# Attention with a gated mixture of experts on one core: the exact path decided from the weights, rows and logits in one product, gates by tanh, first scores inside the prologue

## The chip, the cores and the metric

The kernel runs on one core of one Trainium2 chip. The metric is the device time of one execution in microseconds (us); lower is better. Engines are named as in the profile: PE (matrix products and transposes), ACT (activations), DVE and POOL (vector work), SP (starts most DMAs). A tile name such as `exps` is the program's own.

## What is computed

`x` has 4 batches of 1024 tokens of 128 numbers. With `xn = layernorm(x)`:

```python
p = xn @ Wv.T + bv                      # 16 heads of 8; queries = keys = values = p
s = softmax(p_h @ p_h.T / sqrt(8)) @ p_h  # per batch and head, heads joined
s = s @ Wo.T + bo
z = layernorm(xn)
w = top 2 of softmax(z @ rW + rb), scaled to sum 1     # 8 experts
mixed = sum_e w[e] * (gelu(z @ W1[e] + b1[e]) @ W2[e] + b2[e])   # 128 -> 256 -> 128
out = x + s * silu(xn + mixed)
```

## The kernel before, in words

**The steps.** The 64 pairs of a batch and a head are done four heads at a time: 16 units. A unit has 2 halves of the queries (512 columns) and 8 tiles of 128 keys, so 16 steps, 256 steps in all. In a step PE computes scores (`scores`, L1142: four products into one of three PSUM pairs, two heads each), ACT takes their exponential (L686, two instructions of 128x1024), and PE multiplies by the values of the step two steps back (`values`, L1154). DVE turns and divides each finished half.

**The table of uses.** All other PSUM work goes through one bank, `bank_f`, and a table (`timetable`) says in which step PE makes which use of it: `turn` and `project` of a finished unit, `count` (how many tokens ahead chose the same expert), `bias`, `up` (first layer of four slots of tokens), `down` (second layer). A step has at most one use, but for a *burst*: right after the gelu of a half of the tokens, eight `down` uses stand in a single step. `MOE_AT`, the step of the first `up`, is 31. `GELU_AT`, `GATHER_AT`, `SILU_AT` and `Y_AT` follow from the table: the steps at which ACT does the gelus, POOL starts to fetch expert outputs, ACT does the silus, and DVE finishes a unit's output.

**The prologue.** Before the first step, eight blocks of 512 tokens go through a chain: DVE computes mean and inverse root (`norm1`, a chain of small instructions in which each waits for the one before), ACT normalises (L627), PE transposes (`turn_x`, L1066), ACT copies, PE multiplies by `Wv` (`project_p`, L1073) and by the router (L1078, logits), ACT adds the bias (L642), PE transposes back (`turn_p`, L1086) and sums squares per head (L1092). POOL splits each block into a high and a low part (`split`, L575 square, L578 cast, L580 subtract), and SP stores the parts and the squared norms `m_blk` to `p_dram` (L406, L408), from where `load_head` and `load_stabiliser` (L391 to L398) bring four heads into `k_ring` and `q_ring`, five DMAs a head. DVE copies the rows (L743, `keep_p`) and reduces the norms to a maximum (L746); ACT halves them (L648).

**The exact path.** The score of a token with itself, half its squared norm, serves as the bound that keeps the exponential small. When the largest squared norm `m2` passes 400, a loop computes true row maxima instead. `m2` is known after the last block (L784); PE, DVE and SP then each load it into a register and branch over that loop (PE L1108).

**Routing.** After the branch DVE scales the logits with the second layernorm's factor (`norm2`, `keep_logits` L763), picks the two experts and ranks the tokens (L839 to L855). PE's `count` in step 3 (L1183) waits for that, ACT's small exponential (L677) in step 2 for a part of it. POOL then scatters the tokens' rows to `z_dram`, SP loads expert weights and gathers 512 rows at a time into `z_ring` (L490).

**The queue of SP** is in program order: loads, then per block stores and head loads, then the branch, then at fixed steps whatever the table says.

## Time and profile before

| | us |
|---|---|
| median of 3 runs | 654.75 (652.24 to 656.18) |
| the profiled execution, its own time | 647.5 |
| its span | 645.5 |
| PE busy | 582.8 (90% of the span) |
| ACT busy | 547.7 (85%) |
| DVE busy | 237.8 (37%) |
| POOL busy | 156.7 (24%) |
| mean granted PE clock, share of full | 0.917 |
| first exponential of the first step | 72.69 after the span's start |

Times inside the span are counted from its start. Busy shares are means over stages with different limits: PE is not busy at its peak where its clock is halved, and an engine that is busy beside another may cost nothing. An idle time in a row is put in brackets with what ended it; "issue" is time in which the profile shows no wait.

### The profile page before, as it was taken

The page shows a single profiled execution, that of the slowest core. Times are in us where ns is not written, and L with a number is a line of the kernel's source. Part 1 is how long each engine was busy: PE and PEld are TensorE (multiplying, and loading weights), DVE is VectorE, ACT ScalarE, POOL GpSimd, SP SyncE. Part 2 cuts the span into 40 slices and gives each one's busy share as a digit, 9 for nine tenths or more (in the row PEclk, how much of TensorE's full clock was granted, in tenths as well). Part 3 has the DMA queues.
Part 4 walks back from the last instruction along what each step waited for, and adds up shares of the span by engine and source line. Part 5 has one row for each costly group of instructions (what it writes and reads, how often), then busy time and mean ns, then how long its engine had stood idle before and what let it go on. Part 6 is the DMA issues. An engine that isn't in the chain of part 4 may idle for free.

```text
span 645.5 us, 11510 instructions
## 1 busy us (share of the span) xinstructions
PE 582.8 (90%) x4036; PEld 243.4 (38%) x4036; DVE 237.8 (37%) x677; ACT 547.7 (85%) x595; POOL 156.7 (24%) x172
## 2 busy tenths in 40 slices
PE   5668599979999996999999999999799979999976
PEld 5445142324433444443434343433434434323311
DVE  7555567613333331132222222222234434224323
ACT  2453589959998999799999999999789989999994
POOL 5335147777400000000000000005256000077300
PEclk9856589979999996799999999999589989999978
DMA  7125698765565443435334635333175436232101
GB/s 223 42 81 152 224 302 272 231 170 154 131 155 138 111 100 101 130 77 140 103 98 115 156 93 155 75 88 98 38 196 154 140 95 187 66 91 59 34 17 49
DMA packets 103883, 81.33 MB, mean 126 GB/s; under 512 B 51371, under 2 KB 95806, under 8 KB 103230
## 3 DMA queue, kind: packets, MB, share of 16 engines
q1 hardware_dynamic: 99726, 72.16, 41.3%
q0 software_dynamic: 4096, 8.40, 4.6%
q8 instruction: 33, 0.54, 0.3%
q14 instruction: 28, 0.23, 0.1%
HBM read 57.97 MB, written 28.32 MB: 134 GB/s over the span
## 4 chain that ended last, share of the span: by engine, by line
PE 67%; ACT 14%; DVE 7%; issue 7%; SPq 4%; DMA 1%; ACTq 0%; DVEq 0%
PE bank_v L1154 30%; PE pair L1142 14%; ACT exps L686 11%; PE bank_f L1200 9%; PE bank_f L1191 7%; PE bank_f L1171 1%; PE pair L1073 1%; DVE rows_in_sb L720 1%; SPq L467 1%; PE bank_f L1078 1%; DVE veps L725 1%; PE bank_f L1167 1%; SPq L468 1%; DVE o_ring L990 1%; ACT xn_tok L627 1%
## 5 line engine op out<-in xcount | busy, mean ns | idle before, releaser
L686 ACT ACTIVATE exps<-pair 128x1024 f32<-128x1024 f32 x512 | 487.6, 1050 | 49.6 <-PE pair L1142 31.1
L1154 PE MATMUL bank_v<-exps,v_tok 128*32 128x512 f32 x2048 | 281.7, 623 | 2.2 <-DVE o_turned L946 1.5
L1142 PE MATMUL pair<-q_ring,k_ring 26*128 26x512 f32 x1024 | 155.5, 510 | 13.9 <-ACT exps L686 8.7
L602 POOL DMA_INDIRECT rows_in_sb<-o_dram,dest_i x64 | 60.7, 948 | 372.8 <-DMA o_dram<-o_ring 336.0
L1142 PEld LDWEIGHTS pair<-q_ring,k_ring 26*128 26x128 f32 x1024 | 61.9, 186 | 113.2 <-ACT exps L686 71.2
L1200 PE MATMUL bank_f<-w_ring,pre 128*128 128x128 f32 x320 | 65.5, 334 | 11.7 <-DVE o_ring L990 6.2
L1200 PEld LDWEIGHTS bank_f<-w_ring,pre 128*128 128x128 f32 x320 | 48.6, 218 | 72.1 <-issue 40.8
L592 POOL DMA_INDIRECT z_dram<-pre,dest_i x64 | 64.2, 1003 | 40.8 <-DVE dest_i L909 21.7
L1191 PEld LDWEIGHTS bank_f<-zT,w_ring 128*128 128x128 f32 x320 | 42.5, 193 | 75.2 <-DVE pre L981 45.1
L981 DVE TENSOR_TENSOR pre<-bank_f,w_ring 128x256 f32<-128x256 f32 x80 | 33.9, 424 | 98.5 <-PE bank_f L1191 98.5
L1154 PEld LDWEIGHTS bank_v<-exps,v_tok 128*32 128x32 f32 x2048 | 41.3, 110 | 68.7 <-ACT exps L686 38.0
L1191 PE MATMUL bank_f<-zT,w_ring 128*128 128x128 f32 x320 | 57.6, 304 | 7.1 <-issue 6.2
L990 DVE TENSOR_TENSOR o_ring<-bank_f,w_ring 128x128 f32<-128x128 f32 x80 | 23.3, 291 | 109.6 <-PE bank_f L1200 108.6
L946 DVE STREAM_TRANSPOSE o_turned<-bank_v 128x512 f32<-128x512 f32 x32 | 22.9, 717 | 92.2 <-PE bank_v L1154 92.2
L627 ACT ACTIVATE xn_tok<-x_tok,shift,rstd 128x128 f32<-128x128 f32 x32 | 13.1, 480 | 12.2 <-DVE shift L727 12.2
L648 ACT ACTIVATE pre<-bank_v 16x512 fp32r<-16x512 f32 x8 | 4.7, 585 | 16.8 <-DVE max_block L746 16.8
L666 ACT ACTIVATE pre<-pre 128x2048 f32<-128x2048 f32 x10 | 18.2, 1896 | 0.0
L1066 PE MATMUL pair<-ident,xn_tok 128*128 128x128 f32 x32 | 7.1, 361 | 12.0 <-ACT xn_tok L627 12.0
L926 DVE STREAM_TRANSPOSE zT<-z_ring 128x512 f32<-128x512 f32 x20 | 14.2, 712 | 9.4 <-DMA z_ring<-z_dram 8.7
L964 DVE TENSOR_TENSOR s_tok<-bank_f,bo_bc 128x256 f32<-128x256 f32 x16 | 6.8, 424 | 27.3 <-PE bank_f L1171 27.3
L575 POOL TENSOR_TENSOR pre<-pre 128x512 bf16<-128x512 f32 x8 | 8.3, 1043 | 33.5 <-ACT pre L642 25.3
L956 DVE COPY attnT<-bank_f 128x256 f32<-128x256 f32 x16 | 6.8, 425 | 25.3 <-PE bank_f L1167 25.3
(130 smaller groups left out, 306.3 us busy)
## 6 DMA issues: line engine op xcount, KB each, us to landing
w_ring<-w_dram SPq DMA_DIRECT2D x80, 192.0 KB
w_ring<-w_dram SPq DMA_DIRECT2D x80, 129.0 KB, 2.1
q_ring<-p_dram SPq DMA_DIRECT2D x56, 104.0 KB
k_ring<-p_dram SPq DMA_DIRECT2D x56, 96.0 KB
z_dram<-s_tok SPq DMA_DIRECT2D x4, 1280.0 KB, 8.7
z_ring<-z_dram SPq DMA_DIRECT2D x80, 64.0 KB
o_dram<-o_ring SPq DMA_DIRECT2D x20, 256.0 KB, 2.3
p_dram<-pre SPq DMA_DIRECT2D x16, 256.0 KB, 2.9
```

Of the source, the lines that this page charges most:

```text
L592: pool.indirect_dma_start(z_dram[h][:, :], bass.IndirectOffsetOnAxis(dest_i[:, h, c, i:i + 1].bitcast(U32), 0), z0[:, h * HT + i, :], None ...
L602: pool.indirect_dma_start(rows_in_sb[:, (h * HT + i) % GATHER_RING, c, :], None, o_dram[h][:, :], bass.IndirectOffsetOnAxis(dest_i[:, h, c ...
L627: ins = nc.scalar.activation(xn_tok[:, t, :], x_tok[:, t, :], ACT.Identity, bias=shift[:, t:t + 1], scale=rstd[:, t:t + 1])
L666: nc.scalar.activation(part, part, ACT.Gelu).then_inc(gelu_done, 1)
L686: nc.scalar.activation(exps[:, g % ES, 2 * half:2 * half + 2, :], pair[(2 * g + half) % 3][:, :, :], ACT.Exp, scale=SCALE).then_inc(exp_do ...
L946: nc.vector.transpose(o_turned[:, qh, :, :], bank_v[:, :].rearrange("p (r s) -> p s r", s=QR)).then_inc(o_turned_ready, 1)
L981: ins = nc.vector.tensor_tensor(pre[:, k, i * HF:(i + 1) * HF].rearrange("p (c t) -> p c t", c=FC), bank_f[:, 0:HF].rearrange("p (c t) -> ...
L990: ins = nc.vector.tensor_tensor(o_ring[:, q % 2, i, :], bank_f[:, 0:D], w2_ring[:, q % 2, i, FC * D:W2W], ALU.add)
L1142: ins = nc.tensor.matmul(pair[h % 3][:, j % 2, :], k_ring[32 * j:32 * j + KROWS, n % 2, kt * P:(kt + 1) * P], q_ring[32 * j:32 * j + KROWS ...
L1154: ins = nc.tensor.matmul(bank_v[32 * j:32 * j + 32, :], v_tok[:, (n // HG) * KT + kt, first:first + 32], exps[:, g % ES, j, :], start=(kt ...
L1191: ins = nc.tensor.matmul(bank_f[:, c * P:(c + 1) * P], w1_ring[:, q % 2, i, c * P:(c + 1) * P], zT[:, q % 2, i * P:(i + 1) * P], start=Tru ...
L1200: ins = nc.tensor.matmul(bank_f[:, 0:D], pre[:, k, (i * FC + c) * P:(i * FC + c + 1) * P], w2_ring[:, q % 2, i, c * D:(c + 1) * D], start= ...
```

## The change

- **The decision.** The largest squared norm is bounded from the weights: PE multiplies `Wv` with itself per head and adds the bias's product, DVE sums absolute values per row (`sum_gram`), PE transposes, DVE takes the maximum (`keep_m2`). PE decides and branches before the first block; the usual prologue stands in the `Else` part. DVE and SP load the same number and branch where they did. For the given weights the largest half row sum is 1.11 and the limit 1.535.
- **Rows and logits in one product.** `rows_p` multiplies the transposed block with `Wv` and the router side by side (128 columns of rows, 8 of logits), four products a block; `turn_p` and the separate logits go. DVE adds the bias (L785) and keeps the logits (L786). The norms' sums (`norms_p`) come three blocks later, and DVE copies them (`keep_n2`) where it reduced and ACT halved.
- **First scores inside the prologue.** The first three score groups stand between the last products of the prologue.
- **Fills.** ACT fills `k_ring` and the zeros where POOL did; POOL's square of a block no longer waits for the sums of the block before.
- **Loads.** All 20 head loads go in a row at block 2, and W1 (1 MB) with two small loads behind the norms of block 3 instead of at the start. `norm2` of both halves moves behind the last `keep_n2`. The 16 tiles of the last `norm1` are cut in two times 8.
- **Table.** First `up` at step 36, bursts of six `down` with two more placed apart; gelus at 87 and 182 (before 81 and 174), fetches at 176 and 228 (170 and 220).
- **Gates.** silu(u) becomes u(1 + tanh(u/2))/2: eight tanh of four tiles each, at steps 187, 192, 198, 204, 239, 244, 250 and behind the last step, with one DVE instruction behind each (`gate`), in place of two silus of 16 tiles at 198 and 248. Units 14 and 15 are both finished behind the last step; before, only 15 was.

```diff
-M2_LIMIT = 400.0
+N2_LIMIT = 400.0
+M2_LIMIT_BITS = int(np.float32(0.99 * N2_LIMIT / (D + 1) / 2).view(np.int32))
-NORMS = ((0, 4), (4, 4), (8, 8), (16, 16))
-WARM = (9, 8)
+NORMS = ((0, 4), (4, 4), (8, 8), (16, 8), (24, 8))
+WARM = (4, 6)
-MOE_AT = 31
+MOE_AT = 36
-BURST = 2
+BURST = 6
...
-        uses[g] = [("down", first + k, i) for k in range(BURST) for i in range(4)]
+        downs = [("down", first + i // 4, i % 4) for i in range(8)]
+        uses[g] = downs[:BURST]
...
+        t = g + 3
+        for what in downs[BURST:]:
+            t = max(t, place(what, t) + 1 - MOE_STEP) + MOE_STEP
...
                 sp.wait_ge(parts_ready, g + 1)
...
+                if g == 2:
+                    for i in range(2):
+                        sp.wait_ge(parts_stored[i], 16 * PARTS)
+                    sp.wait_ge(m_kept[0], 32)
...
+                    for j in range(4):
+                        load_head(0, 0, j, 0, kq_in[0])
+                        load_stabiliser(0, j, kq_in[0])
                 sp.wait_ge(n2_copied, g + 1)
...
+                if g == 3:
+                    sp.dma_start(w1_stage, W1.rearrange("e h f -> h e f")).then_inc(w1_staged, 16)
...
-            pool.memset(k_ring[:, :, :].bitcast(F32), 1.0).then_inc(ring_cleared, 1)
-            pool.memset(s_tok[:, :, :], 0.0).then_inc(zeros_ready, 1)
...
-            def silu(h):
-                act.wait_ge(combined, (h + 1) * HT)
-                part = xn_tok[:, h * HT:(h + 1) * HT, :]
-                nc.scalar.activation(part, part, ACT.Silu).then_inc(gate_ready, 1)
+            def tanh_half(c):
+
+                act.wait_ge(combined, (c + 1) * SILU_TILES)
...
+                nc.scalar.activation(th[:, c % 2, :], part, ACT.Tanh, scale=0.5).then_inc(tanh_ready, 1)
...
+            def keep_n2(g):
                 dve.wait_ge(n2_mm, g + 1)
-                nc.vector.tensor_reduce(max_block[:, g:g + 1], bank_v[0:H, :], X, ALU.max).then_inc(n2_max, 1)
+                nc.vector.tensor_copy(m_blk[:, g, :].bitcast(F32R), bank_v[0:H, :]).then_inc(n2_copied, 1)
...
+            keep_n2(0)
+            norm1(4, *NORMS[4])
+            for g in range(3, NB):
                 keep_p(g)
...
+                keep_n2(g - 2)
+            for g in range(NB - 2, NB):
+                keep_n2(g)
+            for h in range(HALVES):
+                norm2(h)
...
+            with pe.Else():
+                keep_warm(WARM[1])
+                prologue()
+                first_scores(0)
+                rows_p(NB - 1)
+                norms_p(NB - 3)
+                first_scores(1)
+                norms_p(NB - 2)
+                first_scores(2)
+                norms_p(NB - 1)
```

PE at the end of the prologue, before: the last block's way back and its sums (L1092), the transpose of the maxima (L1105, behind DVE's last reduction), the load of `m2` and the branch; the first scores stand behind the skipped loop.

```order
L1086 MATMUL pair<-ident,pre 128x128 [waits p_copied,pT_copied]
L1086 MATMUL pair<-ident,pre 128x128 x3
L1092 MATMUL bank_v<-pre,head_sel 16x512 [waits n2_max,n2_copied,sq_ready]
L1105 MATMUL pair<-ident,max_head 1x16 [waits p_copied,max_head_ready]
L1107 TENSOR_LOAD m [waits m2_ready]
L1108 COMPARE_AND_BRANCH
```

PE at the same place in the change (L1130 projects the last block, L1139 is rows and logits, L1146 the norms' sums, L1179 the scores, in three groups of two heads):

```order
L1130 MATMUL pair<-pre,wv_rw 128x512 [waits pT_copied,xT_copied]
L1179 MATMUL pair<-q_ring,k_ring 128x512 [waits kq_in0,xT_copied]
L1179 MATMUL pair<-q_ring,k_ring 128x512
L1139 MATMUL pair<-wv_rw,pre 128x136 [waits p_copied]
L1139 MATMUL pair<-wv_rw,pre 128x136 x3
L1146 MATMUL bank_v<-w_ring,head_sel 16x512 [waits n2_copied,sq_ready]
L1179 MATMUL pair<-q_ring,k_ring 128x512 [waits pT_copied]
L1179 MATMUL pair<-q_ring,k_ring 128x512
L1146 MATMUL bank_v<-w_ring,head_sel 16x512 [waits n2_copied,sq_ready]
L1179 MATMUL pair<-q_ring,k_ring 128x512 [waits p_copied]
L1179 MATMUL pair<-q_ring,k_ring 128x512
L1146 MATMUL bank_v<-w_ring,head_sel 16x512 [waits n2_copied,sq_ready]
```

The three first score groups moved ahead of the last sums, and between them stand sums that wait for POOL's squares (`sq_ready`) and DVE's copies (`n2_copied`); load and branch are gone from here and stand ahead of the first block.

DVE at the same place, before: `norm2` of the first half (L734 to L738, its middle left out here) stood between the copies of blocks 2 and 3; its last rows and what follows:

```order
L737 TENSOR_TENSOR veps<-veps,rstd 128x16 [waits dve_chain]
L738 TENSOR_TENSOR rstd<-rstd,veps 128x16 [waits dve_chain]
L743 COPY v_tok<-pair 128x4x16x8 [waits p_tr,dve_chain]
L746 TENSOR_REDUCE max_block<-bank_v 16x1 [waits n2_mm]
L734 SCALAR_TENSOR_TENSOR veps<-veps,mv 128x16
L706 TENSOR_SCALAR rstd<-veps 128x16 [waits dve_chain]
```

DVE in the change, from the rows of block 6 to the start of `norm2` (L785 and L786 keep rows and logits, L790 is `keep_n2`, L760 begins `norm2`):

```order
L785 TENSOR_TENSOR v_tok<-pair,rows_in_sb 128x4x16x8 [waits p_mm]
L786 COPY lg_all<-pair 128x32
L790 CAST exps<-bank_v 16x512 [waits n2_mm]
L785 TENSOR_TENSOR v_tok<-pair,rows_in_sb 128x4x16x8 [waits p_mm]
L786 COPY lg_all<-pair 128x32
L790 CAST exps<-bank_v 16x512 [waits n2_mm] x3
L760 SCALAR_TENSOR_TENSOR veps<-veps,mv 128x16
L732 TENSOR_SCALAR rstd<-veps 128x16 [waits dve_chain]
L733 TENSOR_SCALAR rstd<-rstd 128x16 [waits dve_chain]
```

Both chains of `norm2`, 14 instructions each in which every one waits for the one before, stand behind the last three `keep_n2`; the register load and the branch follow them.

SP in the change, from the last two issues of the head loads (L416, L420) on; L428 stores the parts of a block, L439 its norms, L441 is W1:

```order
L416 DMA q_ring<-p_dram 8x1024
L420 DMA q_ring<-p_dram 2x1024
L439 DMA p_dram<-exps 16x512 [waits n2_copied]
L428 DMA p_dram<-z_ring 16x8x512 [waits parts_ready]
L428 DMA p_dram<-o_ring 16x8x512
L439 DMA p_dram<-exps 16x512 [waits n2_copied]
L441 DMA w_ring<-in_L_ffn_W 128x8x256
L442 DMA rb_bc<-in_L_ffn_rb 128x8
L443 DMA bo_bc<-in_L_attn_bo 128x128
L428 DMA p_dram<-z_ring 16x8x512 [waits parts_ready]
L428 DMA p_dram<-o_ring 16x8x512
L439 DMA p_dram<-exps 16x512 [waits n2_copied]
```

Before, one head load of five issues stood behind the stores of each of the blocks 2 to 5, and W1 ahead of all blocks; now the parts of block 3 stand behind all 20 issues, and those of block 4 behind W1 as well.

## Rows read from the trace of the kernel before

**Rows 1.** The page, chain of work that ended last, shares of the span.

```profile
PE 67%; ACT 14%; DVE 7%; issue 7%; SPq 4%; DMA 1%; ACTq 0%; DVEq 0%
```

**Rows 2.** Timeline, PE, first transpose of a block: start us, us, engine, line, op, names, count.

```profile
15.35 0.77 PE L1066 MATMUL pair<-ident,xn_tok 128*128 128x128 f32 x4
```

**Rows 3.** Timeline, DVE, first inverse root, then the statistics of the last 16 tiles.

```profile
4.93 4.77 DVE L725 TENSOR_SCALAR veps<-mv 128x4 f32<-128x4 f32 x1
...
28.50 3.17 DVE L720 BATCH_NORM_STATS2 rows_in_sb<-x_tok 128x6 f32<-128x128 f32 x16
```

**Rows 4.** Timeline, PE, around the branch and the count.

```profile
71.86 1.22 PE L1142 MATMUL pair<-q_ring,k_ring 26*128 26x512 f32 x6 [4.88 <-issue]
...
80.69 0.23 PE L1183 MATMUL bank_f<-pre,earlier 128*128 128x128 bf16 x1
```

**Rows 5.** Timeline, DVE, last norms, first instruction behind the branch, the choice.

```profile
65.88 0.68 DVE L746 TENSOR_REDUCE max_block<-bank_v 16x1 f32<-16x512 f32 x1 [0.35 <-PE bank_v L1092]
...
72.05 0.17 DVE L758 TENSOR_TENSOR rconst<-bank_f,rb_bc 128x8 f32<-128x8 f32 x1 [4.87 <-issue]
...
79.90 0.23 DVE L855 TENSOR_SCALAR pre<-pre 128x128 bf16<-128x128 f32 x1
```

**Rows 6.** Timeline, DVE, first and last of the 14 instructions of a norm2.

```profile
50.79 0.15 DVE L734 SCALAR_TENSOR_TENSOR veps<-veps,mv 128x16 f32<-128x16 f32 x1
...
53.49 0.18 DVE L738 TENSOR_TENSOR rstd<-rstd,veps 128x16 f32<-128x16 f32 x1
```

**Rows 7.** Timeline, POOL, first and last of the three instructions of a split.

```profile
43.27 1.05 POOL L575 TENSOR_TENSOR pre<-pre 128x512 bf16<-128x512 f32 x1 [1.93 <-PE bank_v L1092]
...
44.96 1.28 POOL L580 TENSOR_TENSOR pre<-pre 128x512 fp32r<-128x512 f32 x1
```

**Rows 8.** Timeline, DVE, an instruction of a norm2 beside that split.

```profile
45.15 1.12 DVE L709 SCALAR_TENSOR_TENSOR newton<-rstd 128x16 f32<-128x16 f32 x1
```

**Rows 9.** Timeline, DMA queue of SP: W1 and the last small load.

```profile
7.22 2.52 SPq L369 DMA_DIRECT2D w_ring<-in_L_ffn_W  x1
...
11.41 0.43 SPq L371 DMA_DIRECT2D bo_bc<-in_L_attn_bo  x1
```

**Rows 10.** Timeline, DMA queue of SP: first of five head issues, and the two stores after them.

```profile
45.13 0.30 SPq L391 DMA_DIRECT2D k_ring<-p_dram  x1
...
46.97 1.20 SPq L406 DMA_DIRECT2D p_dram<-pre  x2
```

**Rows 11.** The page, DMA issues: KB each, median us to landing.

```profile
p_dram<-pre SPq DMA_DIRECT2D x16, 256.0 KB, 2.9
```

**Rows 12.** Timeline, PE, ACT and SP around the first up, step 31.

```profile
140.37 1.20 PE L1191 MATMUL bank_f<-zT,w_ring 128*128 128x128 f32 x4 [4.72 <-issue]
...
142.33 1.94 ACT L686 ACTIVATE exps<-pair 128x1024 f32<-128x1024 f32 x2 [5.48 <-PE pair L1142]
145.84 5.17 ACT L686 ACTIVATE exps<-pair 128x1024 f32<-128x1024 f32 x5 [1.57 <-PE pair L1142]
...
135.77 6.50 SPq L490 DMA_DIRECT2D z_ring<-z_dram  x12
```

**Rows 13.** Timeline, ACT and PE, after and in the first burst.

```profile
261.81 1.94 ACT L686 ACTIVATE exps<-pair 128x1024 f32<-128x1024 f32 x2 [3.29 <-PE pair L1142]
...
249.80 1.22 PE L1200 MATMUL bank_f<-w_ring,pre 128*128 128x128 f32 x4 [0.39 <-DVE o_ring L990]
```

**Rows 14.** Groups of ACT by line, 505 to 646 us: count, busy us, mean ns, idle.

```profile
L671 ACT ACTIVATE xn_tok<-xn_tok 128x2048 f32<-128x2048 f32 x2 | 3.8, 1910 | 0.0
L671 ACT ACT_TABLE_LOAD x2 | 2.6, 1283 | 0.0
```

**Rows 15.** Timeline, ACT, first pauses behind the two silus.

```profile
524.80 4.01 ACT L686 ACTIVATE exps<-pair 128x1024 f32<-128x1024 f32 x4 [1.44 <-PE pair L1142]
...
625.58 1.94 ACT L686 ACTIVATE exps<-pair 128x1024 f32<-128x1024 f32 x2 [0.73 <-PE pair L1142]
```

**Rows 16.** Timeline, DVE, first of the two instructions that finish a unit.

```profile
642.37 0.43 DVE L940 TENSOR_TENSOR s_tok<-s_tok,xn_tok 128x256 f32<-128x256 f32 x1
```

More of the change, by code:

```diff
@@ L130, in timetable @@
         t = both("up", k, t)
-    gelu = [burst(0, t)]
-    t = gelu[0] + 2
+    first, t = burst(0, t)
+    gelu = [first]
     t = both("up", QUADS, t)
     t = both("up", QUADS + 1, t)
-    for k in range(BURST, QUADS):
+    for k in range(2, QUADS):
         t = both("down", k, t)
         t = both("up", QUADS + k, t)
-    gelu.append(burst(QUADS, t))
-    t = gelu[1] + 4
-    for k in range(BURST, QUADS):
+    second, t = burst(QUADS, t)
+    gelu.append(second)
+    for k in range(2, QUADS):
         t = both("down", QUADS + k, t)
@@ L259, in build @@
         bank_m = [pair[2][:, i, :] for i in range(2)]
+        p_rows = pair[2][:, :, :].rearrange("p a (t w) -> p (a t) w", w=2 * P)
+        bank_g = [pair[1][:, i, :] for i in range(2)]
         p_dram = nc.dram_tensor("p_dram", [H, HEAD_ROWS, N], F32)
@@ L623, in normalise @@
             def normalise(g):
-                if g != 3 and g <= 4:
-                    act.wait_ge(norm_ready, (1, 2, 3, 3, 4)[min(g, 4)])
+                if (c := {first // TB: c for c, (first, _) in enumerate(NORMS)}.get(g)) is not None:
+                    act.wait_ge(norm_ready, c + 1)
                 for t in range(g * TB, (g + 1) * TB):
@@ L679, in _ @@
                         gelu(h)
-                    if g == SILU_AT[h]:
-                        silu(h)
+                for c in range(SILUS):
+                    if g == SILU_AT[c]:
+                        tanh_half(c)
+                if 2 <= g < 4:
+                    act.wait_ge(m_kept[g - 2], NB // 2 * 16)
                 for half in range(2):
@@ L687, in _ @@
                                          scale=SCALE).then_inc(exp_done, 1)
-            for h in range(HALVES):
-                if SILU_AT[h] >= STEPS:
-                    silu(h)
+            for c in range(SILUS):
+                if SILU_AT[c] >= STEPS:
+                    tanh_half(c)
         @block.vector
@@ L1016, in beside @@
                         scale_w1(part)
+                for c in range(SILUS):
+                    if g == GATE_AT[c]:
+                        gate(c)
                 for n in range(NU - 1):
@@ L1033, in _ @@
                     read_bank(*use)
-            finish_y(NU - 1)
+            for c in range(SILUS):
+                if GATE_AT[c] >= STEPS + VLAG:
+                    gate(c)
+            for n in range(NU):
+                if n == NU - 1 or Y_AT[n] >= STEPS + VLAG:
+                    finish_y(n)
         @block.tensor
@@ L1047, in _ @@
             keep_warm(WARM[0])
[L1048 to L1049 removed]
+            pe.wait_ge(wv_in, 32)
+            nc.tensor.transpose(pair[0][:, 0, 0:D], wv_sb, ident[:, :]).then_inc(wv_tr, 1)
+            pe.wait_ge(wv_copied, 1)
+            nc.tensor.matmul(bank_g[0][:, 0:D], wvT, wvT, start=True, stop=False)
+            nc.tensor.matmul(bank_g[0][:, 0:D], bv_bc[0:1, :], bv_bc[0:1, :], start=False, stop=True).then_inc(gram_mm, 1)
+            pe.wait_ge(rows_in, 16 * 5)
             nc.tensor.transpose(bank_f[:, D:2 * D], wo_sb, ident[:, :])
@@ L1108, in _ @@
             with pe.If(m2_bits > M2_LIMIT_BITS):
+                prologue()
+                rows_p(NB - 1)
+                for g in range(NB - 3, NB):
+                    norms_p(g)
+                pe.wait_ge(p_copied, NB)
                 with pe.Fori(0, NU // 2) as w:
@@ L1131, in _ @@
                 pe.wait_ge(exact_in, NU * 16 * PART_LOADS + 16 * KQ_FIRST)
-            def scores(g, half):
-                n, k = divmod(g, US)
-                qh, kt = divmod(k, KT)
-                h = 2 * g + half
-                if k == 0 and half == 0:
-                    pe.wait_ge(kq_in[n % 2], 16 * (KQ_FIRST + n // 2 * KQ_LOADS))
-                if h >= 3:
-                    pe.wait_ge(exp_done, h - 2)
-                for j in range(2 * half, 2 * half + 2):
-                    ins = nc.tensor.matmul(pair[h % 3][:, j % 2, :], k_ring[32 * j:32 * j + KROWS, n % 2, kt * P:(kt + 1) * P],
-                                           q_ring[32 * j:32 * j + KROWS, n % 2, qh * BLK:(qh + 1) * BLK], start=True, stop=True)
-                ins.then_inc(scores_done, 1)
+                for h in range(3):
+                    first_scores(h)
+            with pe.Else():
+                keep_warm(WARM[1])
+                prologue()
+                first_scores(0)
+                rows_p(NB - 1)
+                norms_p(NB - 3)
[3 more added lines that the diff above has]
+                norms_p(NB - 1)
             def values(g):
@@ L1206, in _ @@
                 if g < STEPS:
-                    scores(g, 0)
-                    scores(g, 1)
+                    for half in range(2):
+                        if 2 * g + half >= 3:
+                            scores(g, half)
                 if g >= VLAG:
```

250 lines of the change are left out of this document (138 added, 112 removed).

## The prediction

> **What bounds the kernel now.** I read the chain of work that ended last first: PE holds two thirds of the span, ACT 14%, and 7% is "issue", waits that nothing in the profile explains [rows 1]. So neither engine is slow as a whole; the loss lies in single holes, and the timelines of PE, ACT, DVE and SP's queue around each idle time show four kinds. (a) The prologue: first transpose of a block at 15.35 [rows 2], last norms read at 66.56 (65.88 + 0.68) [rows 5], then both PE and DVE stand 4.88 and 4.87 us at the branch [rows 4, 5]. (b) Step 31, the first `up`: PE waits 4.72 us and ACT idles 5.48 and 1.57, because SP issued the gather of tokens only from 135.77 [rows 12]. (c) Two bursts, after which ACT idles 3.29 [rows 13]. (d) Two silus with a table load on either side [rows 14].
>
> The durations below come from the profiled execution, 647.5 us, 7.25 (1.1%) under the median 654.75. I put the sum on the median. A difference of 0.5%, 3.3 us, is about what a measurement of this kernel can tell from no change.
>
> **The prologue.** PE must now wait for `m2` before the first block. DVE's first chain was held 4.77 us in its first small instruction [rows 3] while POOL filled the tiles that ACT fills now; without that hold the first two `norm1`, about 4.1 each from 3.6 on, and the small sums between them end near 12.8: `m2`. The branch adds 4.88 [rows 4] and six warming products some 2.6, all estimates from these rows: first transpose at 20.3, 4.9 later than before. That the fills leave POOL gains nothing at the end, since PE's branch is later than the norms either way.
>
> Next, DVE. Before, it reached the statistics of the last tiles at 28.50 [rows 3], 13.2 after the first transpose; now one more slot of PE (about 4, because the norms lag by three blocks) stands ahead, so 37.5. The last `norm1` has 8 tiles: half of 3.17 [rows 3], 0.6 of averages, and a chain of 13 that I take from the 14 of a `norm2`, 50.79 to 53.67 = 2.88 [rows 6]; with one hold by POOL as in [rows 8], 6 us in all: 43.5. Rows of block 3 and norms of block 1 end at 45.2; the store lands about 2 later. Then SP issues 20 loads: five took from 45.13 to 46.97, 1.84 [rows 10], so 7.4, until 54.6. With four landed some 2 later the first scores and exponential come near 57, 15 us earlier than before. That is the gain the eye sees first, and it can't be kept, for the reason that follows.
>
> Behind the loads on SP stand the norms of block 2 (0.6), the parts of block 3 (1.2) and its norms (0.6), each bounded by a store of [rows 10]; then W1 with the two small loads, 7.22 to 11.84 = 4.62 [rows 9]; then the parts of block 4, 0.6 to the issue of the second and 2.9 to landing [rows 11]. That is 65.1. POOL's cast of block 6 waits for it: cast and subtraction 1.92 (a split of 2.97 less its square 1.05 [rows 7]), the square of block 7 1.05, the sums about 0.4 (six products of 512 columns took 1.22 [rows 4]), DVE's copy 0.68 [rows 5], hand-overs 0.2: the last norms are kept at 69.3. Before, at 66.56.
>
> Then, in line on DVE: two `norm2`, before hidden between blocks, now 2 x 2.88 = 5.8; the branch 4.87; routing from 72.05 to 80.13 = 8.08 [rows 5]. The choice is ready at 88.1. ACT's routing exponential, in step 2, and PE's `count`, in step 3, wait for it, and behind them every later score: the hold. Before, PE came to the count at 80.69 [rows 4] with the choice ready. So step 4 starts 7.4 later. PE then has idled for some 10 us. After the idle of step 31 the next pause of ACT was 1.57 [rows 12]; I add that. **Prologue: +9.0.** Bounds: 0 if the choice is ready by 80.7; +13.5 if the parts land 4.5 later (below).
>
> **Step 31.** The first `up` comes at step 36, five steps later; SP's gather, tied to earlier steps, is issued at the same distance from them. Five steps at about 1.9 are 9.5, the wait was 5.48 [rows 12]: 4 us to spare. **-7.0** (5.48 + 1.57). Bounds: 0, if SP falls 4 us behind, and -7.0.
>
> **Bursts.** ACT's 3.29 [rows 13] is waiting for eight `down`. Six leave out two of 1.22 and a pause of 0.39 each [rows 13], 3.2. Those two then take a place in later steps, at most 1.2 each; I take 0.6, since part of it lies beside ACT's exponentials: -2.0 a burst. **-4.0**, bounds 0 and -6.6.
>
> **Gates.** Two silus took 1.91 each, and four table loads (two at L671 and, not shown, two ahead of the next exponential) 1.28 each [rows 14]: 8.9. Behind them ACT idled 1.44 and 0.73 [rows 15]: 11.1 goes. The eight tanh have 512 columns where a silu has 2048: between 0.48, a quarter, and 1.91 [rows 14]; I take 0.6, nearer the quarter. Three in steps that ACT bounds cost 1.8; the first four, where PE sets the pace, some 0.7; the last lies behind the last exponential, beside the last values. **-8.6**; bounds -11.1 and -6.3 (all eight in full). No table load stands beside a tanh in the order of the changed program. DVE's `gate` runs where DVE is mostly idle; if that cover went, each would cost its step at most about 0.9.
>
> **End.** Unit 14 is finished behind the last step too: two instructions of 0.43 [rows 16], and the last gate about 0.2: **+1.1**. The fetches start 8 steps later, and so do their readers; they keep their distance. The one product for rows and logits shortens PE's slots, but the prologue's end is set by SP and DVE: worth 0.
>
> Sum: 9.0 - 7.0 - 4.0 - 8.6 + 1.1 = -9.5. 647.5 becomes 638.0; on the median **645.2**.
>
> **The rivals.**
>
> No hold. If the branches cost little in the change, `m2`'s branch on PE and the one on DVE give 4.8 each back: the choice near 78.5, before PE needs it; prologue 0, time 636.2. Against it: both engines show the wait of 4.9 at the branch [rows 4, 5]; for it: that they waited there over a loop, and the code behind may have been fetched by then. The Trainium skill (Advanced Engine Details and Errata, section Control Flow Timing) gives a compare-and-branch about 108 ns, which is this case. By it the sum would be 636.2; by the trace's 4.88, which I keep, 645.2. A shorter wait of SP in the prologue does the same. Chance 0.15.
>
> W1 in the way. The parts of block 4 are issued behind a megabyte. If they land only once it has, the cast of block 6, the choice and step 4 come later; the small stores' 2.9 [rows 11] then holds no longer. I take one and a half such landings, 4.5, as the price: 649.7. For it: the same queue's order. Chance 0.12.
>
> The stall stays. If SP, which now issues the loads of the first units later, falls 4 us behind, ACT's wait moves to step 36: up to 7.0 back, 652.2. Against it: these loads wait for the steps, not for SP. Chance 0.06.
>
> The lock, the one on the slower side. A DVE instruction of 0.17 took 1.12 beside POOL's subtraction [rows 8]: it ended when POOL's did. In the change every `norm1` of the later tiles, `keep_p` with its two inputs and, if POOL is late, `norm2` run while POOL splits. At worst DVE loses all of POOL's time, 8 x 2.97 [rows 7] less 24 instructions of 0.17 that get through, 19.7; I have counted 1. Then 645.2 + 18.7 = 663.9. It decides the sign when DVE loses more than 13.8 in the chain to the choice (645.2 + 12.8 = 658.0). Against it: POOL waits for blocks in between, and its splits 5 to 7 fall where DVE has only copies. The Trainium skill (SBUF — State Buffer) calls the port pair of DVE and GpSimd an exclusive lock, held for a whole instruction; by that rule the price is the one worked out here, and [rows 8] agrees with 1.12 against 0.17. Chance 0.06.
>
> The exact path is taken after all, so that the change doesn't do what it says: 1.11 against 1.535 leaves no doubt short of a mistake in the bound; no row prices that loop, and the time would be far over 658. Chance 0.01.
>
> **How the numbers follow.** The forecast's chance is 0.60. Its own range: prologue +4 to +12, bursts -6.6 to -2, gates -10 to -7: 637 to 651. For 8 times in 10 it takes in half of "no hold" and "the stall stays" and leaves the lock out: 635 to 653. Faster by over 0.5% (under 651.5): nearly all of the forecast (0.58), no hold (0.15), three quarters of W1 (0.09): 0.82. Within 0.5%: 0.02 + 0.03 + the stall 0.06 = 0.11. Slower: the lock and the exact path, 0.07.
>
> **What would show it.** Right: the first exponential near 57; DVE's last `keep_n2` near 69; two exponentials, then ACT and PE idle until DVE's choice near 88; steps 5 to 9 on the grid of before, about 9 later; no wait at step 36; ACT's pause behind a burst under 0.5; five table loads instead of nine. Wrong: a count made near 80 or earlier means no hold; DVE instructions of 1 us in the chains, the lock; a transpose of `z_ring` that waits for its DMA at step 35, the stall. If the first exponential's lead of 15 us reached step 8, the whole reading of routing as the bound is wrong.

## The result, and the profile after

| | before | changed |
|---|---|---|
| median of 4 runs, us | 653.5 (647.3 to 656.18) | 639.05 (637.87 to 640.63) |
| the profiled execution, its own time | 647.5 | 637.87 |
| its span | 645.5 | 636.1 |
| first exponential of the first step | 72.69 | 57.83 |
| table loads on ACT | 9 | 5 |

The ratio of the comparable runs is 0.985, 95% interval 0.9805 to 0.9895: faster by 1.5%, clear of no change but under 2%. The forecast was 645.2 on a median of 654.75, a ratio of 0.9854, and -9.5 us on the profiled execution; measured there is -9.6 (637.87 against 647.5, again 0.985). As a time, 639.05 is 6 us under 645.2: the forecast put a sum read in an execution of 647.5 on a median of 654.75. The kernel before varies more than the changed one, perhaps because its steps 4 to 7 can run at half clock too (its prologue does so below, in the run with the gates alone), so single medians of it are not subtracted here.

The sum was right; two of its terms were not, and that they cancel is luck. The start of a step's first exponential, read off the timeline of ACT in both kernels, gives where the time went. The steps compute the same; only the uses of the bank beside them move.

| step | before | changed | difference | what lies since the row above |
|---|---|---|---|---|
| 0 | 72.69 | 57.83 | -14.9 | prologue up to the first scores |
| 4 | 81.45 | 87.31 | +5.9 | the hold |
| 16 | 106.74 | 120.54 | +13.8 | half clock in steps 4 to 8 |
| 48 | 176.68 | 182.52 | +5.8 | step 31 |
| 80 | 242.90 | 248.24 | +5.3 | |
| 96 | 291.34 | 293.05 | +1.7 | first burst |
| 168 | 438.03 | 439.71 | +1.7 | |
| 184 | 486.88 | 483.90 | -3.0 | second burst |
| 192 | 503.47 | 501.58 | -1.9 | second burst's downs placed apart (steps 185, 186), first tanh |
| 208 | 541.40 | 534.03 | -7.4 | first silu |
| 240 | 601.53 | 596.13 | -5.4 | later uses, tanh |
| 255 | 634.97 | 624.69 | -10.3 | second silu |
| end of the span | 645.5 | 636.1 | -9.4 | end |

**The prologue and the hold.** PE, timeline of the changed kernel, at its branch, the last sums of norms, the wait for ACT and the wait for the choice (columns as in [rows 2]):

```profile
18.85 2.93 PE L1099 MATMUL bank_v<-ident 128*128 128x128 f32 x12 [7.61 <-issue]
...
69.18 0.59 PE L1146 MATMUL bank_v<-w_ring,head_sel 128*16 128x512 bf16 x1 [5.55 <-POOL w_ring L597]
...
81.97 0.79 PE L1179 MATMUL pair<-q_ring,k_ring 26*128 26x512 f32 x2 [8.46 <-ACT exps L712]
...
86.17 0.26 PE L1267 MATMUL bank_f<-pre,earlier 128*128 128x128 bf16 x1 [1.54 <-DVE pre L893]
...
87.20 1.93 PE L1238 MATMUL bank_v<-exps,v_tok 128*32 128x512 f32 x8
89.06 1.87 PE L1262 MATMUL bank_f<-cols,w_ring 128*128 128x1 f32 x8
```

The first row answers to [rows 2]: PE's first work behind the branch comes at 18.85. The count stands at 86.17, 5.5 later than in [rows 4]. In the last two rows a step's four products of the values take 1.93 and its four bias products 1.87 (the program issues four of each; the trace has two records for each). In the kernel before, at full clock, the same took 1.07 and 1.05:

```profile
81.35 1.07 PE L1154 MATMUL bank_v<-exps,v_tok 128*32 128x512 f32 x8
82.34 1.05 PE L1178 MATMUL bank_f<-cols,w_ring 128*128 128x1 f32 x8
```

DVE, timeline of the changed kernel: the last norms, the first of the two `norm2`, the first instruction behind the branch, the choice:

```profile
69.81 0.68 DVE L790 CAST exps<-bank_v 16x512 fp32r<-16x512 f32 x1 [5.89 <-PE bank_v L1146]
70.42 0.65 DVE L760 SCALAR_TENSOR_TENSOR veps<-veps,mv 128x16 f32<-128x16 f32 x1
...
77.99 0.17 DVE L801 TENSOR_TENSOR rconst<-bank_f,rb_bc 128x8 f32<-128x8 f32 x1 [1.28 <-issue]
...
85.80 0.23 DVE L893 TENSOR_SCALAR pre<-pre 128x128 bf16<-128x128 f32 x1
```

Against [rows 5]: the line is the one forecast, with the two chains (70.42 to 76.71) in it, but load and branch cost 1.28 where they cost 4.87.

POOL, timeline of the changed kernel, the cast of block 6:

```profile
66.18 0.61 POOL L600 CAST z_ring<-zT 128x512 fp32r<-128x512 f32 x1 [3.41 <-DMA p_dram<-o_ring]
```

It waits for the stored parts of block 4, as forecast. SP had issued W1 and, behind it, the last of them:

```profile
57.92 0.42 SPq L441 DMA_DIRECT2D w_ring<-in_L_ffn_W  x1
...
60.20 0.60 SPq L428 DMA_DIRECT2D p_dram<-o_ring  x1
```

**The clock.** Granted clock (PEclk) of the changed kernel around the restart; columns: stretch, length, busy time and count of PE, PEld, DVE, ACT, POOL, then PEclk, DMA share, GB/s:

```profile
82.00:93.00 11.00, 9.46 (x44) 3.36 (x44) 8.15 (x21) 5.91 (x7) 0.00 (x0) 0.50 0.86 246
93.00:104.00 11.00, 11.00 (x52) 6.31 (x48) 4.99 (x15) 4.51 (x5) 5.25 (x5) 0.50 0.94 305
104.00:120.00 16.00, 15.39 (x101) 4.15 (x101) 11.20 (x27) 14.43 (x17) 12.34 (x13) 0.87 0.43 121
```

The same view of the kernel before, at its steps 4 to 7:

```profile
81.00:92.00 11.00, 11.00 (x88) 5.57 (x92) 9.55 (x32) 8.51 (x9) 2.95 (x2) 0.94 0.90 259
```

Between 93 and 104 PE is busy all the time, at 0.50, the lower of its two levels, and has 52 records of products; before, in as long a stretch at 0.94, 88. Steps 4 to 7 take 4.39 us each (87.31, 91.69, 96.09, 100.49) where they took 2.41 (81.45 to 88.70). ACT shows it as pauses, timeline of the changed kernel:

```profile
91.69 1.94 ACT L712 ACTIVATE exps<-pair 128x1024 f32<-128x1024 f32 x2 [2.45 <-PE pair L1179]
```

**Step 36, bursts, gates.** From the page of the changed kernel: DVE's transposes of the gathered rows, which the first `up` waits for, had 0.7 us of idle time before them in all (before, 9.4, of which 8.7 for DMA):

```profile
L964 DVE STREAM_TRANSPOSE zT<-z_ring 128x512 f32<-128x512 f32 x20 | 14.2, 712 | 0.7
```

ACT, timeline of the changed kernel, behind the first burst; the pause of 3.29 of [rows 13] is gone:

```profile
273.63 3.87 ACT L712 ACTIVATE exps<-pair 128x1024 f32<-128x1024 f32 x4
278.16 3.77 ACT L712 ACTIVATE exps<-pair 128x1024 f32<-128x1024 f32 x4 [0.66 <-PE pair L1179]
```

ACT's groups by line, 440 to 637 us: the eight tanh in place of [rows 14]; the two table loads left there are the second gelu's:

```profile
L694 ACT ACTIVATE z_ring<-xn_tok 128x512 f32<-128x512 f32 x8 | 5.8, 727 | 0.0
L686 ACT ACT_TABLE_LOAD x1 | 1.3, 1283 | 0.0
L712 ACT ACT_TABLE_LOAD x1 | 1.3, 1283 | 0.0
```

### The profile page after: what moved, and what is told of

Its sections match the earlier page's. It is cut to its first block, busy times and chain, and to the rows that moved or that the text cites. A ratio compares the mean times of both kernels' runs of the same rounds, so it can differ in the third digit from the quotient of the medians.

```text
span 636.1 us, 11439 instructions
## 1 busy us (share of the span) xinstructions
PE 571.2 (90%) x3994; PEld 234.0 (37%) x3994; DVE 244.5 (38%) x709; ACT 542.5 (85%) x591; POOL 152.1 (24%) x170
## 4 chain that ended last, share of the span: by engine, by line
PE 66%; ACT 12%; DVE 8%; issue 5%; SPq 5%; DMA 2%; POOL 0%; ACTq 0%; DVEq 0%
PE bank_v L1238 32%; PE pair L1179 15%; ACT exps L712 9%; PE bank_f L1284 8%; PE bank_f L1275 7%; ACT pre L686 1%; PE bank_f L1255 1%; PE bank_f L1262 1%; DMA p_dram<-o_ring 1%; SPq L493 1%; DVE newton L736 1%; DVE rows_in_sb L746 1%; SPq L494 1%; DVE o_turned L992 1%; SPq L516 1%
## 5 line engine op out<-in xcount | busy, mean ns | idle before, releaser
L1179 PE MATMUL pair<-q_ring,k_ring 26*128 26x512 f32 x1024 | 155.1, 510 | 11.9 <-ACT exps L712 9.9
L1179 PEld LDWEIGHTS pair<-q_ring,k_ring 26*128 26x128 f32 x1024 | 61.8, 186 | 107.2 <-ACT exps L712 66.1
L1284 PEld LDWEIGHTS bank_f<-w_ring,pre 128*128 128x128 f32 x320 | 45.7, 206 | 71.4 <-issue 45.8
L1284 PE MATMUL bank_f<-w_ring,pre 128*128 128x128 f32 x320 | 61.9, 320 | 9.6 <-ACT pre L686 5.2
L1238 PEld LDWEIGHTS bank_v<-exps,v_tok 128*32 128x32 f32 x2048 | 41.3, 110 | 69.3 <-ACT exps L712 38.3
L1139 PE MATMUL pair<-wv_rw,pre 128*128 128x136 f32 x64 | 10.2, 308 | 8.4 <-DVE lg_all L786 8.4
L1139 PEld LDWEIGHTS pair<-wv_rw,pre 128*128 128x128 f32 x64 | 9.6, 214 | 13.7 <-DVE lg_all L786 10.5
L1255 PEld LDWEIGHTS bank_f<-woT,attnT 128*128 128x128 f32 x64 | 8.7, 198 | 13.3 <-issue 5.9
```

The costliest lines, as they stand in the source:

```text
L1139: ins = nc.tensor.matmul(p_rows[:, t, 0:TW], xnT[:, g % 2, t * P:(t + 1) * P], wv_rw[:, :], start=True, stop=True)
L1179: ins = nc.tensor.matmul(pair[h % 3][:, j % 2, :], k_ring[32 * j:32 * j + KROWS, n % 2, kt * P:(kt + 1) * P], q_ring[32 * j:32 * j + KROWS ...
L1238: ins = nc.tensor.matmul(bank_v[32 * j:32 * j + 32, :], v_tok[:, (n // HG) * KT + kt, first:first + 32], exps[:, g % ES, j, :], start=(kt ...
L1284: ins = nc.tensor.matmul(bank_f[:, 0:D], pre[:, k, (i * FC + c) * P:(i * FC + c + 1) * P], w2_ring[:, q % 2, i, c * D:(c + 1) * D], start= ...
```

## The experiments

Time and ratio below are against the kernel before, run on the same chip beside each; spans against the changed kernel's 636.1.

**1. Both norm2 ahead of the last two keep_n2.**

```diff
-            for g in range(NB - 2, NB):
-                keep_n2(g)
             for h in range(HALVES):
                 norm2(h)
+                keep_n2(NB - 2 + h)
```

> The changed kernel with both norm2 chains moved ahead of the last two keep_n2, into pauses in which DVE waits for POOL (2.9 and 5.9 us in its timeline). Theory: the choice of experts is late because the two norm2 stand behind the last keep_n2 (70.42 to 76.71); moved, the choice ends 5.8 earlier, near 80.3, and the hold of 5.5 us against the kernel before is gone: 5.5 us faster at least. If the half clock of the steps behind the hold (4.39 us a step where before it was 2.41) comes from PE's idling in the hold, it shortens too, by up to 8 more: 5.5 to 13.5 faster. Rival: the chains, now beside POOL's splits, lose 1 us at each of POOL's instructions, and the gain falls to 2 to 3 us; or the clock stays low because of the bias products of steps 4 to 7, and the gain is 5.5 and no more.

635.05 us, ratio 0.9773 (0.9738 to 0.9808), span 633.4. Step 2 began at 77.57 instead of 80.92, and steps 4 to 7 still took 4.39 each (83.97 to 97.14). The line to the choice was what held the steps; the gain of 3.0 at step 16 is at the rival's number, and the half clock did not care for a shorter hold.

**2. The biases four steps later.**

```diff
-BIAS_AT = 4
-SCALE_W1_AT = (8, 10, 11, 12)
+BIAS_AT = 8
+SCALE_W1_AT = (12, 14, 15, 16)
```

> The changed kernel with the four bias uses at steps 8 to 11 (before 4 to 7) and the scaling of W1 four steps later. Theory: behind the hold PE restarts at half clock and returns to full only some time after, whatever it does; then steps 4 to 7 cost 2.6 instead of 4.39 at half clock, but some of the bias products still meet the half clock at steps 8 to 11: 2 us faster or less. Rival: it is the bias products, short and with one column, that keep the clock low; without them it is full again by step 7, steps 4 to 7 save 7 and steps 8 to 11 cost 2.4 more: 4 to 5 us faster, and the half clock ends before 95 instead of 105.

632.67 us, ratio 0.9717 (0.9671 to 0.9763), span 632.9. The hold was the same (step 4 at 87.92), but steps 4 to 7 went 2.60, 2.59, 1.82, 1.81. Granted clock in that run:

```profile
82.00:93.00 11.00, 8.88 (x40) 1.90 (x40) 9.76 (x25) 7.15 (x8) 0.00 (x0) 0.50 0.90 263
93.00:104.00 11.00, 11.00 (x92) 5.14 (x92) 5.25 (x17) 9.59 (x11) 7.58 (x8) 0.97 0.93 293
```

Full from 93 on, where the changed kernel stayed at 0.50 until 108. In its mechanism the rival is right: with the bias products behind the restart the clock stayed down, without them it rose. The gain was 3.2 in the spans and 6.4 in the medians, for its 4 to 5. Step 8 came 8.1 earlier; of that the bias uses in steps 8 to 11, and a half clock that they met from 104 on, took back 4.9 by step 16.

**3. PE kept busy through the hold.**

```diff
                 if g == 0:
                     pe.wait_ge(n2_copied, NB)
                     pe.wait_ge(consts_ready, CONSTS)
+                    keep_warm(28)
```

> The changed kernel with 28 products of the identity with itself (12 us at half clock, less at full) ahead of the first values, in the time in which PE waits for the routing. They compute nothing that is used. Theory that the idling lowers the clock: PE comes out of the hold at full clock, steps 4 to 8 take 2.4 instead of 4.39, 6 to 8 us faster. Rival that the bias products hold the clock down: no gain, or up to 2 us lost, since the added products end only near 83 at half clock.

639.57 us, ratio 0.9836 (0.9799 to 0.9873), span 638.4. Granted clock in that run:

```profile
77.00:87.00 10.00, 6.75 (x55) 4.32 (x53) 8.06 (x20) 3.96 (x5) 0.00 (x0) 0.99 0.78 290
87.00:107.00 20.00, 19.35 (x90) 9.74 (x94) 10.41 (x34) 8.40 (x9) 6.30 (x6) 0.50 0.85 255
```

The extra products did bring the clock to full by 77. But PE then waited for the choice again, and the clock fell in that wait, before the first bias product (the stretch just before the count, and the count):

```profile
86.00:87.00 1.00, 0.00 (x0) 0.00 (x0) 0.98 (x1) 0.14 (x1) 0.00 (x0) 0.87 0.92 228
```

```profile
87.65 0.27 PE L1268 MATMUL bank_f<-pre,earlier 128*128 128x128 bf16 x1 [2.70 <-DVE pre L893]
```

The bias steps met half clock as in the changed kernel and took 4.39 each. So this run did not keep PE busy through the hold, and it doesn't separate the idling from the bias products; experiments 2 and 11 do.

**4. W1 at the start again.**

```diff
             for c in range(2, len(X_CHUNKS)):
                 load_x(c)
+            sp.dma_start(w1_stage, W1.rearrange("e h f -> h e f")).then_inc(w1_staged, 16)
...
-                if g == 3:
-                    sp.dma_start(w1_stage, W1.rearrange("e h f -> h e f")).then_inc(w1_staged, 16)
...
```

> The changed kernel with W1 and the two small loads issued at the start again, behind the loads of x. Theory: the parts of block 4 (landed some 5 us after their last issue) and of block 3 wait behind W1's megabyte and the three issues; without them POOL's casts of blocks 6 and 7 come 2 to 4 us earlier, so does the last keep_n2 (69.81), and the kernel is 2 to 4 us faster. Rival: W1 then delays the loads of x or the zeros, the first blocks come later, and nothing is gained or 1 to 2 us are lost.

635.03 us, ratio 0.9765 (0.9735 to 0.9796), span 633.2; the last norms were kept at 66.25 instead of 69.81 (DVE in that run):

```profile
66.25 0.68 DVE L789 CAST exps<-bank_v 16x512 fp32r<-16x512 f32 x1 [2.21 <-PE bank_v L1145]
```

The megabyte did stand in the way of the parts; the first exponential stayed where it was (57.93).

**5. The first up at step 31 again.** (`MOE_AT = 36` to `31`.)

> The changed kernel with the first up at step 31 again. Theory: SP's gather, issue-bound, comes 30 us after the loads of unit 2 whatever the table says, so PE waits about 5 us at step 31 again and ACT's pauses add up to 5 to 7: 5 to 8 us slower than the changed kernel. Rival: SP's queue moved with the steps differently in the change, or the 8 us that the steps from 24 to 40 gained came from elsewhere: slower by 2 us or less.

649.12 us, ratio 0.9975 (0.9934 to 1.0016), span 646.8, 10.7 more than the changed kernel. ACT and SP in that run:

```profile
158.41 1.94 ACT L712 ACTIVATE exps<-pair 128x1024 f32<-128x1024 f32 x2 [7.69 <-PE pair L1179]
```

```profile
151.45 6.83 SPq L516 DMA_DIRECT2D z_ring<-z_dram  x12
```

The gather was issued at 151.45; the changed kernel issued its own at 151.42. The wait is SP's, whatever step the table names: 8.1 by step 32. The other 2 to 3 us came between steps 32 and 48 and at the second burst, and weren't followed up.

**6. Eight downs in a burst.** (`BURST = 6` to `8`.)

> The changed kernel with eight downs in a burst, none placed apart. The forecast has 2 us a burst: 4 us slower. By the steps of the two traces the bursts gave 3.6 and 4.7, 8 us slower, if the table's later uses have no part in that. Rival: the eight downs were hidden anyway and the gain came from where the gelus stand: no difference.

645.41 us, ratio 0.9913 (0.9875 to 0.9951), span 642.5: 6.4 for two bursts, 3.2 each. ACT behind the first burst in that run:

```profile
273.47 1.94 ACT L712 ACTIVATE exps<-pair 128x1024 f32<-128x1024 f32 x2
278.75 1.94 ACT L712 ACTIVATE exps<-pair 128x1024 f32<-128x1024 f32 x2 [3.34 <-PE pair L1179]
```

The pause of [rows 13] is back to its size, and for the first burst, whose gelu stands at step 87 in both, it is the whole price: 3.4 us by step 96. The second burst (the table now has its gelu at step 180 instead of 182) took 4.8 more by step 184, of which 1.1 came back by step 187, where the changed kernel has its two downs placed apart.

**7. The kernel before with the gates alone changed.**

```diff
-SILU_AT = (COMBINE_AT[0][-1] + 2, min(COMBINE_AT[1][-1] + 2, STEPS))
+SILU_AT = [COMBINE_AT[c * SILU_TILES // HT][c * SILU_TILES % HT + SILU_TILES - 1] + 2 for c in range(SILUS)]
...
-                nc.scalar.activation(part, part, ACT.Silu).then_inc(gate_ready, 1)
+                nc.scalar.activation(z_ring[:, c % 2, :], part, ACT.Tanh, scale=0.5).then_inc(tanh_ready, 1)
```

> The kernel before with the gates alone changed: eight tanh with one DVE instruction each, and the outputs of units 14 and 15 finished at the end, at the steps that its own table gives (nothing else). Forecast: the silus' 11.1 us go, the tanh cost 2.5, the end 1.1: 7.5 us faster than the kernel before. Rival: a tanh costs its step more than its 0.6 us, since the waits for DVE's combine and gate stand in ACT's queue: 3 to 5 faster.

Its four executions took 636.11 to 651.08 us, too far apart for a ratio; the profiled one took 647.85. Its steps still tell two things. With the prologue of the kernel before, unchanged, its steps 4 to 7 take 4.39 each (ACT, timeline of this run):

```profile
86.73 1.94 ACT L693 ACTIVATE exps<-pair 128x1024 f32<-128x1024 f32 x2 [2.45 <-PE pair L1165]
```

so that it was 10.8 behind the kernel before from step 16 to step 176. From there to the last step it gained 10.3 (480.54 against 469.70, 635.51 against 634.97). Of that, 1.2 came between steps 176 and 179, ahead of the first tanh (step 181), so the gates gave 9.1 up to the last step, and the end cost nothing (10.4 from the last step to the end of the span, 10.6 before): more than the 7.5 expected. And the half clock of the bias steps is not the changed kernel's own: the prologue of the kernel before can fall into it as well.

**8. Edits 1, 2 and 4 together.**

> The changed kernel with three edits of the runs before together: both norm2 ahead of the last keep_n2, the biases at steps 8 to 11, W1 at the start. Alone they gave 3.3, 3.1 and 3.3 us in the traces. Theory: the first and the third shorten the same line to the choice one after the other, the second acts on the clock behind it: they add, 9 to 10 faster than the changed kernel. Rival: once the choice comes earlier than PE needs it the rest is lost, or the earlier steps meet another wait (heads of unit 1, W1's scaling): 5 to 7 faster.

627.16 us, ratio 0.9675 (0.9589 to 0.9762), span 624.7, 11.4 under the changed kernel. They add, and a little more: bias steps 9 to 12 stayed at 2.41. DVE in that run, first and last instruction of the first `norm2`, beside POOL's splits of blocks 5 to 7 (59.19 to 66.99):

```profile
59.86 0.15 DVE L759 SCALAR_TENSOR_TENSOR veps<-veps,mv 128x16 f32<-128x16 f32 x1
...
67.68 0.17 DVE L763 TENSOR_TENSOR rstd<-rstd,veps 128x16 f32<-128x16 f32 x1
```

8.0 us for what [rows 6] show as 2.88.

**9. The norm2 ahead of the rows of block 7.**

```diff
             for g in range(3, NB):
+                if g == NB - 1:
+                    for h in range(HALVES):
+                        norm2(h)
                 keep_p(g)
```

> The three edits together, but both norm2 ahead of the rows of block 7 instead of ahead of the last two keep_n2. There DVE waited 3.5 us for PE while POOL waited for a store. In the run with the three edits the first norm2 took 8.0 us (59.86 to 67.85) instead of 2.88, beside POOL's splits. Theory of the lock: in the pause of POOL both chains take their 2.9 each, the last keep_n2 ends near 67 instead of 72, and the kernel is 4 to 5 us faster than with the three edits. Rival: the later rows of block 7 hold back PE's scores and the last norms, and 1 us or less is gained.

628.2 us, ratio 0.9667 (0.958 to 0.9755), span 626.1. DVE in that run, the first chain from first to last, then the first and last of the second:

```profile
55.83 0.15 DVE L759 SCALAR_TENSOR_TENSOR veps<-veps,mv 128x16 f32<-128x16 f32 x1
...
58.53 0.17 DVE L763 TENSOR_TENSOR rstd<-rstd,veps 128x16 f32<-128x16 f32 x1
58.74 0.17 DVE L759 SCALAR_TENSOR_TENSOR veps<-veps,mv 128x16 f32<-128x16 f32 x1
...
63.88 1.12 DVE L763 TENSOR_TENSOR rstd<-rstd,veps 128x16 f32<-128x16 f32 x1
```

With POOL idle the first took 2.87; the second, which ran into the splits, 6.3. Its last row, 1.12 where the first chain has 0.17, ended at 65.00, and the subtraction of POOL's that ran beside it (63.68 and 1.28 long) at 64.96. The Trainium skill (SBUF — State Buffer, section Terms) calls the port pair of DVE and GpSimd an exclusive lock, held for a full instruction; these rows agree. The choice came 3.1 earlier than in run 8 (step 4 at 79.54 against 82.59). It was lost again: the bias steps fell to half clock here (step 11 took 4.38), and at step 16 the two runs are level, 109.01 and 108.80.

**10. Routing's waits two steps later.**

```diff
-COUNT_AT = (3, 20)
+COUNT_AT = (5, 20)
...
-EXP_AT = (2, 15)
+EXP_AT = (4, 15)
```

> The run before, with the first routing exponential at step 4 instead of 2, the first count at step 5 instead of 3, and what follows the count two steps later. Theory: what stands in the way of the first scores is only the place of these two waits, so that two more steps go before the choice is ready: 2 to 4 us faster than the run before. Rival: the steps then wait for the norms' stores or the choice itself, or the scatter, two steps later, is late for the first up: no gain.

628.55 us, ratio 0.9664 (0.9573 to 0.9755), span 626.7. The first half did as the theory says: step 16 at 100.55, 8.5 ahead of run 9 (its bias steps stayed at full clock). All of it was lost at step 36. PE and SP in that run:

```profile
144.55 1.19 PE L1275 MATMUL bank_f<-zT,w_ring 128*128 128x128 f32 x4 [5.87 <-issue]
```

```profile
121.93 7.97 SPq L404 DMA_DIRECT2D w_dram<-in_L_ffn_b  x8
...
139.81 4.28 SPq L515 DMA_DIRECT2D z_ring<-z_dram  x8
```

The wait of [rows 12] again, one stage later.

**11. No bias products.** DVE takes `b1` alone; the products of the learned shift with W1 are left out, so this kernel computes something else.

```diff
-                    for at in range(4):
-                        e, c = divmod(arg[0] * 4 + at, FC)
...
+                    pe.sem_inc(bank_f_written, 1)
+                    return
```

> The changed kernel without the 16 products of the learned shift with W1 (their uses of the bank stay, without products; DVE takes b1 alone). Theory that these products hold the clock at half behind the hold: full clock some 7 to 10 us after the count, steps 4 to 7 take 2.6 and then 1.8 instead of 4.39: 9 to 11 us faster than the changed kernel, of which 2.4 is their own time at full clock. Rival that the clock comes back only at 105 after such a hold: steps 4 to 8 at 2.6 throughout, 6 to 8 us faster, and the half clock ends where it did.

628.56 us, ratio 0.9678 (0.9599 to 0.9756), span 626.7, 9.4 under the changed kernel. The hold was the same (step 4 at 87.34), the steps behind it 2.59, 2.39, 1.82, 1.81, the clock full by 92:

```profile
92.00:104.00 12.00, 11.90 (x86) 3.38 (x82) 9.67 (x32) 11.69 (x13) 7.82 (x7) 1.00 0.87 283
```

With the same hold and the same half clock at its end, the clock was full 6 us after the count. Of the 9.4, 2.4 are the products' own time at full clock (steps of 2.41 in the kernel before against 1.81 here, four times). So some 7 of the 8 us behind the hold come of the bias products that stand there, and not of the length of the hold.

**12. Run 10 with the second layer's bias in one DMA.**

```diff
-                for e in range(E):
-                    sp.dma_start(w2_dram[e, :, FC * D:W2W], b2[e:e + 1, :].broadcast_to([P, D])).then_inc(w2_kept, 16)
+                sp.dma_start(w2_dram[:, :, FC * D:W2W], b2.rearrange("(e a) d -> e a d", a=1).broadcast_to([E, P, D])).then_inc(w2_kept, 16)
```

> The run with the late count and one edit more: SP writes the second layer's bias to w2_dram with one DMA instead of eight. In that run PE came to step 36 six microseconds earlier than in the run before it and waited 5.9 there for the gather (issued from 139.81), behind eight issues that took 8.0 on SP. Theory that the wait at the first up is SP's queue, whatever the step: the gather is issued 6 to 7 us earlier, the wait goes, 5 to 7 us faster than the run with the late count, near 622. Rival: one DMA of eight times the size takes as long to issue, or the gather waits for POOL's scatter: no gain.

622.53 us, ratio 0.9587 (0.9525 to 0.9648), span 621.2. The time is as expected, the reason isn't. SP in that run:

```profile
123.93 3.50 SPq L403 DMA_DIRECT2D w_dram<-in_L_ffn_b  x1
128.81 10.13 SPq L492 DMA_DIRECT2D w_ring<-w_dram  x8
138.98 4.28 SPq L514 DMA_DIRECT2D z_ring<-z_dram  x8
```

The issue took 3.50 instead of 7.97, but the loads behind it took 10.13 (8.55 in run 10), and the gather went out only 0.8 earlier. The wait was gone because this execution's bias steps fell to half clock and PE came to step 32 at 136.76 instead of 130.36. The rest of its lead over run 10, 2.0 at step 48 and 5.1 at the last step, grew around the bursts; why wasn't tested. It is the fastest version here, 4.1% under the kernel before.

## Why the prediction was right, and where it was not

**Step 31: right.** -7.0 forecast, -8.0 between steps 16 and 48 (-8.5 up to step 80), and undone it costs 8.1 at the place [experiment 5]. The margin was there, but nearer 2 us than 4: in experiment 5, where SP issued the gather at the same time, the transpose that waits for it began at 155.64; in the changed kernel it began at 157.62, without a wait. Run 10, whose steps came earlier, used the margin up.

**Gates: right.** -8.6 forecast with +1.1 at the end, so -7.5. In the changed kernel the steps gained 8.4 from step 187, where the first tanh stands, to the last, and the end cost 0.9: -7.5. Alone (experiment 7) the gates gave 9.1. A tanh took 0.73 on average, not 0.6; around the two silus 10.4 of the 11.1 came back.

**Bursts: mechanism right, size off.** -4.0 forecast; -7.2 by the steps (from step 80 to step 192), 6.4 when undone (experiment 6). Two terms were mis-sized. For "those two then take a place in later steps ... I take 0.6" each, 1.2 a burst, nothing shows at the first burst and 1.1 at the second; and eight downs in place of six cost 3.4 and 4.8, where the sum has 3.2.

**Prologue: the line right, the restart wrong.** First exponential at 57.83 for "near 57"; the last norms kept at 70.5 for 69.3; the choice at 86.0 for 88.1; the hold 5.5 for 7.4. Two errors ahead of the last norms nearly cancel. W1's issue took 0.42 where I had 2.52, from a row taken right behind the loads of x, and with the two small loads 1.6 for 4.62. But the parts landed 6.0 after the start of their last issue, not 2.9: the rival "W1 in the way" was true as well, at 3.6 by step 4 and 3.1 by step 16 (experiment 4), for its price of 4.5.

The branch is a third error, and half of the rival "no hold" came true with it: 1.28 on DVE for 4.87, 3.96 on PE for 4.88 (`m2` at 14.89, the next work at 18.85). What I priced as a branch has three parts. Views of the branch's own line in the changed kernel (count, duration in ns, start):

```profile
L832 DVEq COMPARE_BRANCH  x1: 72/72/72, 77.3 to 77.3; - x1
```

```profile
L1185 PEldq COMPARE_BRANCH  x1: 3309/3309/3309, 15.5 to 15.5; - x1
```

On DVE the load of `m2` into the register took 0.55 and the branch 0.07, and before 0.54 and 0.07; what fell is the time from the branch to the next instruction, 4.18 before and 0.59 now. On PE the branch itself is long, 3.31 and 3.88 before. The Trainium skill (Advanced Engine Details and Errata, section Control Flow Timing) gives a compare-and-branch about 108 ns; DVE's own 72 ns are near it, PE's 3309 are not, and on DVE that is not where the wait was.

The step that failed is "After the idle of step 31 the next pause of ACT was 1.57; I add that": the restart cost 8.3 (13.8 at step 16, less 5.5), since what follows the hold is not a step like the others but four bias steps. The sum has no term for what the clock does in them: at half clock, where the restart leaves PE, they take 4.39 each for 2.41. Experiments 2 and 11 show that it is these steps: moved or left out, the clock is full some 6 us after the count. Experiment 7 shows that they need no hold for it. The prologue's 13.8 lies outside the forecast's own range of +4 to +12. (The bounds given for that range add up to 636 to 652, not 637 to 651.)

So the sum stood by luck: +4.8 in the prologue against -1.5 in step 31 and -3.2 in the bursts, with the gates and the end as forecast. The **lock** was no bound of the changed kernel behind its last norms, as judged (its two norm2 stood behind POOL's last splits), but it was what limited experiment 1, where the two chains beside the splits took 3.8 and 6.3 instead of 2.88 each.

## What to carry to other kernels

A gain ahead of a fixed dependence is worth only what the dependence lets through: 15 us of earlier scores were held by a choice that came 5.5 later, and it paid to shorten the line to the choice first (runs 1, 4 and 8). When work is moved so that PE restarts in front of other products than before, read the granted clock of exactly those steps, in more than one execution if there is one. A wait that goes because its consumer came later is not gone: in experiment 10, with the steps before it 8 us earlier, the gather's wait came back.

## What was not expected

In the changed kernel the clock stayed at half from before the count to about 108, through all four bias steps, with PE busy all the time from 87 on. Where the bias steps began at full clock, it fell too: in the middle of them in experiments 9 and 12, ahead of the last in experiment 2, and right behind them for 2 to 3 us in experiment 8 and in the kernel before (0.50 between 92 and 94). Only in experiment 10 did it stay full. What decides between these wasn't found.

Load and branch past a loop cost DVE 4.87 before, 1.28 in the changed kernel and about 0.9 in runs 9 and 10; PE's, past a longer body, 3.96. What makes the difference wasn't tried.
